# Edge stage of a graph layer: one-hots become the stationary operand of the node sums, messages go in as two exact halves

## What is computed

```
xn   = layernorm(x)
msg  = relu(xn[src] + edge_attr @ W_edge + b_edge)        # 50000 x 256
agg  = segment_sum(msg, dst)                               # 3125 x 256
h    = (1 + eps) * xn + agg
h    = relu(h @ W1 + b1) @ W2 + b2, batch norm, relu
q, k = elu(xn @ Wq.T) + 1, elu(xn @ Wk.T) + 1;  v = xn @ Wv.T
mix  = (q @ (k.T v)) / (q @ sum(k)), projected             # 8 heads
x    = x + h + mix
x    = x + routed_ffn(layernorm(x))                        # 2 of 8 experts per node
```

## Time and profile before

| | |
|---|---|
| median of 3 runs | 1014.85 us (1013.4 to 1015.24) |
| the profiled execution's own time | 1009.37 us |
| its span from first to last instruction | 1007.6 us |
| edge stage, first fetch to `edges_done` | 43.0 to 559.6 us |
| graph layer's rest, routing | 559.6 to about 680 us |
| feed-forward blocks | about 680 us to the end |

### The profile page before, as it was taken

How to read it: one execution, slowest core, us unless ns; L and a number is a source line. 1 busy time by engine, 2 the same in 40 slices (tenths; PEclk the granted TensorE clock), 3 DMA queues, 4 the chain that set the end, 5 groups by cost and what they waited for, 6 DMA issues and landing times.

```text
span 1007.6 us, 17432 instructions
## 1 busy us (share of the span) xinstructions
PE 926.4 (92%) x6055; PEld 824.6 (82%) x6055; DVE 601.8 (60%) x1098; ACT 538.3 (53%) x1064; POOL 544.6 (54%) x527
## 2 busy tenths in 40 slices
PE   5899999999999999999999975379999999999995
PEld 4677889889888888897888765368999999999994
DVE  5555665565665565568989778835554454555442
ACT  2744545445545455445545564836555666555552
POOL 3277777777777777777774004023444444444433
PEclk8899999999999999999999998589999999999998
DMA  9667888877878878799775105459799789888722
GB/s 247 198 165 231 264 259 266 254 253 251 277 243 260 274 252 262 249 304 324 248 241 184 43 1 182 168 201 384 236 312 308 239 289 301 279 253 301 244 42 28
DMA packets 93173, 234.59 MB, mean 233 GB/s; under 512 B 20425, under 2 KB 37843, under 8 KB 84122
## 3 DMA queue, kind: packets, MB, share of 16 engines
q1 hardware_dynamic: 56694, 116.95, 33.9%
q0 software_dynamic: 29136, 64.72, 26.5%
q10 hardware_dynamic: 7252, 51.75, 12.8%
HBM read 183.81 MB, written 50.23 MB: 232 GB/s over the span
## 4 chain that ended last, share of the span: by engine, by line
PE 59%; POOL 13%; DMA 10%; DVE 8%; issue 7%; ACT 2%; DVEq 0%; POOLq 0%; SPq 0%; ACTq 0%
PE banks L1154 15%; POOL work L775 13%; PE banks L1174 10%; DMA work<-node_table,srcT 8%; PE banks L476 7%; PE banks L450 7%; PE banks L1176 5%; PE banks L924 3%; PE banks L983 2%; PE banks L439 2%; PE banks L1063 2%; PE banks L1051 1%; DVE work L526 1%; PE banks L1138 1%; DMA wts<-in_src 1%
## 5 line engine op out<-in xcount | busy, mean ns | idle before, releaser
L775 POOL DMA_INDIRECT work<-node_table,srcT x391 | 382.9, 979 | 151.6 <-issue 109.8
L498 ACT ACTIVATE work<-work 128x512 f32<-128x512 f32 x195 | 120.9, 630 | 127.0 <-DVE work L526 126.3
L476 PEld LDWEIGHTS banks<-work 128*128 128x128 f32 x1560 | 184.2, 192 | 4.5 <-DVE hT L544 1.1
L476 PE MATMUL banks<-work 128*128 128x128 f32 x1560 | 184.8, 275 | 0.7 <-DVE hT L544 0.7
L450 PE MATMUL banks<-w_edge,eaT 128*128 128x256 f32 x780 | 179.1, 379 | 0.0
L526 DVE TENSOR_TENSOR work<-banks,work 128x512 f32<-128x512 f32 x195 | 128.0, 682 | 69.5 <-DMA work<-node_table,srcT 55.1
L824 POOL DMA_INDIRECT out<-work,row_i x54 | 86.5, 1601 | 141.5 <-ACT work L1444 118.9
L1154 PE MATMUL banks<-xe_hi,wup 128*128 128x256 f32 x864 | 158.8, 285 | 3.8 <-DVE xe_lo L1901 3.8
L450 PEld LDWEIGHTS banks<-w_edge,eaT 128*128 128x128 f32 x780 | 143.1, 190 | 17.0 <-issue 0.2
L1174 PE MATMUL banks<-wdown,hid_hi 128*128 x432 | 155.9, 403 | 0.0
L1909 DVE TENSOR_TENSOR hid_lo<-wts,hid_hi 128x512 fp32r<-128x512 f32 x108 | 72.4, 691 | 134.7 <-ACT hid_hi L1421 134.7
(11 more groups left out here) (258 smaller groups left out, 1199.1 us busy)
## 6 DMA issues: line engine op xcount, KB each, us to landing
wup<-split_table ACTq DMA_DIRECT2D x24, 2048.0 KB, 9.7
work<-in_edge_attr SPq DMA_DIRECT2D x65, 384.0 KB, 5.1
wts<-in_L_ffn_W SPq DMA_DIRECT2D x64, 256.0 KB, 4.6
split_table<-raw_hi SPq DMA_DIRECT2D x64, 256.0 KB, 2.6
split_table<-raw_lo SPq DMA_DIRECT2D x64, 256.0 KB, 4.2
wdown<-split_table SPq DMA_DIRECT2D x8, 2048.0 KB, 9.7
work<-node_table,srcT POOLq DMA_INDIRECT x391, 4.5
wup<-split_table SPq DMA_DIRECT2D x3, 2048.0 KB, 8.2
```

The source lines that it names most:

```text
L476: last = nc.tensor.matmul(bank[5][:, h * P:(h + 1) * P], msg[:, u, j, h * P:(h + 1) * P], onehot[:, u, j], start=(j == 0), stop=(j == GT - 1))
L498: nc.scalar.activation(msg[:, u, 2 * q:2 * q + 2], msg[:, u, 2 * q:2 * q + 2], ACT.Relu).then_inc(msg_ready, 1)
L775: pool.indirect_dma_start(out=xg[i % RING][0:rows, j % 2], out_offset=None, in_=node_table, in_offset=bass.IndirectOffsetOnAxis(ap=srcT[0: ...
```

## The change

A one-hot tile is now the stationary operand and the messages of a tile (256 values wide) are the moving one. Both are in the fp32r format: the one-hots are exact in it, and the messages are given as two halves. ACT's relu writes a rounded `msg_hi` to other memory (that of `xs`, which is free in this stage), and a new DVE instruction `low_messages` computes `msg_lo = max(msg, 0) - msg_hi` over the whole group, once ACT is done with all three pairs. PE then runs 12 matmuls of 128x256 (one record each) for a group in place of 24 records of 128x128. The sums now come out node by node where `hT` wants them turned, so ACT copies them to `sums` (`copy_sums`) and PE transposes them (`turn_sums`, two 128x128) before DVE adds them. On ACT the copy of the sums and the mixer's steps come ahead of the edge copy; on DVE `mix_q` comes right behind the one-hots, and `add_window` between the second and the third pair. The loads of x, 10 DMAs, move on SP from n = 51 to 55 to behind `edges_done`, since `xs` now holds messages.

```diff
-        onehot = view(work, 7680, 2, GT, P)
+        msg_lo = nc.alloc_sbuf_tensor_at("msg_lo", [P, 2, GT, DIM], F32R, offset=work_offset + 4 * 4608)
+        msg_hi = nc.alloc_sbuf_tensor_at("msg_hi", [P, 2, GT, DIM], F32R, offset=xs_offset)
+        sums = xs[:, 12]
+        onehot = nc.alloc_sbuf_tensor_at("onehot", [P, 2, GT, P], F32R, offset=work_offset + 4 * 7680)
...
-        def aggregate_tail(pe, n, u):
-            pe.wait_ge(agg_read, n)
-            pe.wait_ge(onehot_ready, n + 1)
-            pe.wait_ge(msg_ready, PAIRS * (n + 1))
-            for h in range(HALVES):
-                last = nc.tensor.matmul(bank[5][:, h * P:(h + 1) * P], msg[:, u, 0, h * P:(h + 1) * P], onehot[:, u, 0],
-                                        start=True, stop=True)
-            last.then_inc(agg_ready, 1)
-
-        def aggregate(pe, n, u, fresh=False):
+        def aggregate(pe, n, u, fresh=False, tiles=GT):
             if not fresh:
                 pe.wait_ge(agg_read, n)
             pe.wait_ge(onehot_ready, n + 1)
+            pe.wait_ge(msg_low, n + 1)
+            for j in range(tiles):
+                for m in (msg_hi, msg_lo):
+                    last = nc.tensor.matmul(bank[5][:, 0:DIM], onehot[:, u, j], m[:, u, j],
+                                            start=(j == 0 and m is msg_hi), stop=(j == tiles - 1 and m is msg_lo))
+            last.then_inc(agg_ready, 1)
+
+        def turn_sums(pe, n):
+            pe.wait_ge(sums_copied, n + 1)
             for h in range(HALVES):
-                for j in range(GT):
-                    if h == 0 and j % 2 == 0:
-                        pe.wait_ge(msg_ready, PAIRS * n + j // 2 + 1)
-                    last = nc.tensor.matmul(bank[5][:, h * P:(h + 1) * P], msg[:, u, j, h * P:(h + 1) * P], onehot[:, u, j],
-                                            start=(j == 0), stop=(j == GT - 1))
-            last.then_inc(agg_ready, 1)
+                last = nc.tensor.transpose(bank[5][:, DIM + h * P:DIM + (h + 1) * P], sums[:, h * P:(h + 1) * P], ident[:])
+            last.then_inc(turned, 1)
...
+        def copy_sums(act, n):
+            act.wait_ge(agg_ready, n + 1)
+            nc.scalar.copy(sums, bank[5][:, 0:DIM]).then_inc(sums_copied, 1)
+
+        def high_tail(act, n, u):
             act.wait_ge(sums_done, PAIRS * (n + 1))
-            nc.scalar.activation(msg[:, u, 0], msg[:, u, 0], ACT.Relu).then_inc(msg_ready, PAIRS)
-
-        def relu_messages(act, n, u):
+            nc.scalar.activation(msg_hi[:, u, 0], msg[:, u, 0], ACT.Relu).then_inc(msg_high, PAIRS)
+
+        def high_messages(act, n, u):
             for q in range(PAIRS):
                 act.wait_ge(sums_done, PAIRS * n + q + 1)
-                nc.scalar.activation(msg[:, u, 2 * q:2 * q + 2], msg[:, u, 2 * q:2 * q + 2], ACT.Relu
-                                     ).then_inc(msg_ready, 1)
+                nc.scalar.activation(msg_hi[:, u, 2 * q:2 * q + 2], msg[:, u, 2 * q:2 * q + 2], ACT.Relu
+                                     ).then_inc(msg_high, 1)
+
+        def low_messages(dve, n, u, tiles=GT):
+            dve.wait_ge(msg_high, PAIRS * (n + 1))
+            nc.vector.scalar_tensor_tensor(out=msg_lo[:, u, 0:tiles], in0=msg[:, u, 0:tiles], scalar=0.0,
+                                           in1=msg_hi[:, u, 0:tiles].bitcast(F32), op0=ALU.max, op1=ALU.subtract
+                                           ).then_inc(msg_low, 1)
...
-        def add_nodes(dve, n, u):
-            for q in range(PAIRS):
+        def add_nodes(dve, n, u, pairs=range(PAIRS)):
+            for q in pairs:
...
-            dve.wait_ge(agg_ready, n + 1)
+            dve.wait_ge(turned, n + 1)
...
+            nc.vector.tensor_tensor(w, bank[5][:, DIM:2 * DIM].rearrange("p (h c) -> p h c", h=HALVES),
...
-                c = n - 2 * TILES - 1
-                if 0 <= c < CHUNKS:
-                    for d, s in node_rows(a["x"], xs[:, c * CHUNK_TILES:(c + 1) * CHUNK_TILES], c):
-                        sp.dma_start(s, d).then_inc(x_again, 16)
...
             sp.wait_ge(edges_done, 1)
+            for c in range(CHUNKS):
+                for d, s in node_rows(a["x"], xs[:, c * CHUNK_TILES:(c + 1) * CHUNK_TILES], c):
+                    sp.dma_start(s, d).then_inc(x_again, 16)
...
+                if n >= 2:
+                    turn_sums(pe, n - 2)
                 if n == DEN0:
                     attn_weights()
-                if n >= 1:
-                    aggregate(pe, n - 1, (n - 1) % 2, n == 1)
                 if n < 2 * TILES:
                     if n % 2 == 0:
                         mix_kv(n // 2)
...
                     context_transpose()
                 if n >= DEN0 and (n - DEN0) % 2 == 0 and (n - DEN0) // 2 < COL_CHUNKS:
                     attn_den((n - DEN0) // 2)
+                if n >= 1:
+                    aggregate(pe, n - 1, (n - 1) % 2, n == 1)
                 if n >= DEN0 + 3 and (n - DEN0 - 3) % 2 == 0:
                     attn_out((n - DEN0 - 3) // 2)
-            aggregate_tail(pe, GROUPS - 1, (GROUPS - 1) % 2)
+            turn_sums(pe, GROUPS - 2)
+            aggregate(pe, GROUPS - 1, (GROUPS - 1) % 2, tiles=1)
+            turn_sums(pe, GROUPS - 1)
...
+            act.wait_ge(rows_ready, CHUNKS)
             for n in range(GROUPS):
-                if n + 1 < GROUPS:
-                    copy_group(n + 1)
+                if n >= 2:
+                    copy_sums(act, n - 2)
                 if 1 <= n <= 2 * TILES:
                     if n % 2 == 1:
                         mix_kv(n // 2)
                     else:
                         mix_q(n // 2 - 1)
+                if n + 1 < GROUPS:
+                    copy_group(n + 1)
                 if n == DEN0:
...
-                    relu_messages(act, n, n % 2)
+                    high_messages(act, n, n % 2)
                 else:
-                    relu_tail(act, n, n % 2)
+                    high_tail(act, n, n % 2)
...
-                    add_window(dve, n - 2, starts[(n - 2) % GT], mixed_by(n + 1), n == 2)
+                    dve.wait_ge(agg_ready, n - 1)
                 if last:
                     mark_tail(dve, n % 2)
                 elif n < 2 or n > 2 * TILES:
...
                     mark_from_psum(dve, n, n % 2)
                 if n % 2 == 1 and n < 2 * TILES:
                     mix_k(n // 2)
+                if n % 2 == 0 and 2 <= n <= 2 * TILES:
+                    mix_q(n // 2 - 1)
                 if n == 2 * TILES:
                     mask_context()
                 c, late = (n - DEN0 - 1) // 2, (n - DEN0 - 1) % 2
                 if 0 <= c < COL_CHUNKS and not last:
                     attn_inverse(c, 2 * late)
+                if not last:
+                    add_nodes(dve, n, n % 2, range(PAIRS - 1))
+                if n >= 2:
+                    add_window(dve, n - 2, starts[(n - 2) % GT], mixed_by(n + 1), n == 2)
                 if last:
                     add_tail(dve, n, n % 2)
                 else:
-                    add_nodes(dve, n, n % 2)
-                if n % 2 == 0 and 2 <= n <= 2 * TILES:
-                    mix_q(n // 2 - 1)
+                    add_nodes(dve, n, n % 2, (PAIRS - 1,))
                 if n >= 1 and (n - 1) % GT == 0:
                     starts = windows_from(n - 1)
                 if n >= 3:
                     round_low(dve, n - 3)
+                low_messages(dve, n, n % 2, 1 if last else GT)```

On DVE, in the mixer's part of the stage, from the end of one group to the end of the next (an odd n), before. `raw_lo` is the weights' low half, `hT<-banks,hT` the window, `work<-banks,relT` the one-hots, `work<-banks,work` the adds:

```order
L587 TENSOR_TENSOR raw_lo_53<-wts,raw_hi_50 128x512
L1571 SCALAR_TENSOR_TENSOR hT<-qT,eps,hT 128x2x125
L544 ISA
L544 TENSOR_TENSOR hT<-banks,hT 128x2x128
L508 TENSOR_TENSOR work<-banks,relT 128x768
L1584 SCALAR_TENSOR_TENSOR k_t<-ek,banks 125x256
L526 TENSOR_TENSOR work<-banks,work 128x512 x3
L587 TENSOR_TENSOR raw_lo_54<-wts,raw_hi_51 128x512
```

More of the change, by code:

```diff
@@ L1321, in _ @@
                     nc.scalar.copy(w2_hi[:], w2[:]).then_inc(w12_high, 1)
+            for n in range(GROUPS - 2, GROUPS):
+                copy_sums(act, n)
             again = act.value_load(miss_i[0:1, 0:1], min_val=0, max_val=1)
@@ L1651, in _ @@
                     round_low(dve, n - 3)
+                low_messages(dve, n, n % 2, 1 if last else GT)
                 if n == 5:
@@ L1689, in _ @@
                         add_nodes_again(dve, n)
+                        low_messages(dve, n, 0)
                         add_window(dve, n, w * WINDOW, TILES)
```

12 lines of the change are left out of this document (8 added, 4 removed).

## The result

The changed kernel takes **1081.35 us** (median of 4 runs, 1079.66 to 1084.63), the one before on the same chip 1014.12 us (4 runs, 1011.92 to 1015.24): a ratio of 1.067, interval 1.0638 to 1.0701. The forecast was 1082 us. The profiled execution took 1079.66 us with a span of 1077.9 us, 70.3 us more than before.

The account below looks back on a forecast made before the run. The prediction took POOL's fetches, not PE, to bound the edge stage. Its terms 51 + 18 - 2 = +67 us on the profiled 1009.37 us made 1076, and 5.5 us to the median made 1082 us; range 1046 to 1108.

Parts of the forecast that it names:

- The bound: Edge stage: POOL's fetches, one every 1.25 us, set the step; PE, 92% busy, runs beside them.
- What holds the fetches: Edge stage: a DVE instruction with both inputs in SBUF holds up a fetch that would start while it runs.
- the term of +51 us: First part, 51 groups: the pass delays fetches 1.00 us a group, the middle of 0.38 to 1.63; bounds +19 and +83.
- +18 for the fetches: Late part, 14 groups: step rises from 7.92 to 9.2 us, +18 us; bounds +16.5 and +23.
- forecast at -2: Last fetch's start to edges_done: 15.7 us becomes about 13.7 by a sum of links; bounds -3 and 0.
- DVE needs 9.1 us: Late part: DVE's 7.35 us of work a group plus the 1.76 us pass, less 0.05 of overlap.
- Almost no idle time: Late part: a sign that would show the forecast's mechanism, DVE left with almost no idle time.
- order on DVE: Edge stage: the new DVE order, with add_window behind two adds, a link under half a step; no cost counted.
- ACT, PE's savings, the loads of x: ACT's 0.37 us copy covered by idle time, PE's 0.8 us a group saved not counted, x loads hidden: 0.
- Rival C: Edge stage: PE's clock falls after pauses, 0.5 us a group, +32 on top, 1114 us; chance 0.05.
- A: First part: the pass does not hold up fetches, only DVE's late load counts, +14.5, 1029 us; chance 0.10.
- B: Edge stage: PE is the bound and gets faster, at most 14 us gained, 1001 us; chance 0.05.

Follow-up runs that it names:

- in thirds: The changed kernel with the pass as three instructions of 512 elements, one behind the other, every value computed: 1050.68 us, ratio 1.0369.
- with a sixth: The changed kernel with the pass over one tile of six, PE using msg_hi again for the other five: 1029.88 us, ratio 1.0149.
- window first: The changed kernel with the window's add, from group 51 on, ahead of the one-hots and adds: 1079.39 us, ratio 1.0637.
- PE filled: The changed kernel with unused matmuls of 128 columns on PE, five or ten a group, so that it pauses less: 1074.41 us, ratio 1.0608.
- sixth and window first: The changed kernel with the pass over one tile of six and, from group 51 on, the window's add ahead: 1023.99 us, ratio 1.0112.
- new until group 50: The changed scheme for groups 0 to 50, the old scheme without the pass from group 51 on: 1052.3 us, ratio 1.0375.
- before with a pass: The old kernel, x loaded late, plus one instruction like the pass on unused memory for groups 2 to 50: 1047.24 us, ratio 1.035.

## Why the prediction was right, point by point

- **The bound** (fetches, not PE): shown for the first part. PE lost 650 records and the time did not fall; in five kernels with PE's new work and a short, divided or PSUM-side pass a group takes 7.66 to 7.78 us there, close to the old 7.65.
- **What holds the fetches**: shown by three kernels from three sides: the input's place (7.66 us), the instruction's length (7.76 us in thirds, 7.70 with a sixth), the instruction alone (+35.1 us). The Trainium skill (SBUF — State Buffer, "Who interferes with whom") says that a DVE instruction with at most one SBUF input outside its two-port modes does not contend with GpSimd; the PSUM input agrees (0.95 us inside the pass). It also infers that descriptor generation isn't held up by a `tensor_tensor`; these fetches are held up by instructions with two SBUF inputs (0.95 us outside, up to 2.48 us inside). Which part of a fetch is held, the reading of its row numbers from SBUF or the making of descriptors, no run shows.
- **Its size**: the term of +51 us measured +40.7. The surplus is 0.80 us a group, not 1.00. The step that failed is taking the middle because landings spread. Of the fetches that start in a pass of the 66 groups, 43 have surpluses of 0.41 to 0.61 us, 18 have 1.02 to 1.53, and two lie between. In 20 of the first part's 51 groups the fetch starts 1.0 to 1.05 us into the pass, so the pass stands in a certain phase to the fetches, and mostly the favourable one. That this comes from landing, add, high half and pass following each other is argued, not shown.
- **The late part**: +18 for the fetches measured +18.5, but this is partly luck, and the end of the stage, forecast at -2, measured +8.7. Together 25.8 us by DVE's own mark for a forecast of 16. The step that failed is "DVE needs 9.1 us", used as the group's step: as busy time it was nearly right (8.87), but it is the step only if every pause closes. "Almost no idle time" was wrong: the old pauses for ACT and landings did shrink, but new ones for PE came, 1.23 us a group in all. The old step plus the pass would be 8.08 + 1.76 = 9.84 for 10.10 measured, but the pass is not the whole cause. With five sixths of it gone (1.34 us) the step falls by 1.01 us only, from 10.10 to 9.09, and 9.2 of the 25.8 us come back. The window's place gives 7.9 more between two traces, and 8.7 are left. The new order and the new links between PE and DVE, which the prediction put at nothing, thus cost about as much here as the pass or more; the node sums' waits for the window name them, but no run takes the link of copy and turns out alone.
- **The end**: the sum of links there took each link as waiting only for the one before it. (The links add up to 12.5 us, not 12.0, which would still be about -2.) Timeline of the changed kernel there:

```profile
609.81 1.09 DVE L1633 SCALAR_TENSOR_TENSOR wts<-wts,qT 128x896 f32<-128x896 f32 x1
...
610.82 0.95 DVE L515 TENSOR_TENSOR onehot<-iota_f,relT 128x768 fp32r<-128x768 f32 x1
611.69 1.55 DVE L1627 RECIPROCAL wts<-wts 128x224 f32<-128x224 f32 x1
613.15 1.22 DVE L539 TENSOR_TENSOR work<-banks,work 128x512 f32<-128x512 f32 x2
...
614.76 0.39 PE L473 MATMUL banks<-msg_hi,onehot 128*128 128x256 f32 x1 [4.21 <-DVE hT L557]
```

  PE waited 4.2 us for a window that stood behind the norm, one-hots, an inverse and two adds. This is the "order on DVE" that was costed at nothing. With a full pass the price of the window's place does not show (window first: 146.2 for 146.4 us); with a short one it is 7.9 us between two traces.
- **ACT, PE's savings, the loads of x**: nothing, as forecast. ACT's copy made PE wait 0.9 us in the late part and the end.
- **Rival C**: its mechanism came true and its price did not. The clock fell to 0.96 and 0.89 in the two parts. With PE filled it was 0.98 and 0.97, and the median 6.9 us lower, not 32; how much of that is the clock's is open.
- **Rivals A and B**: out. A's first part of 7.65 us is approached (7.66 to 7.78) only when the input is in PSUM or the pass is short or divided; B needed a pass that costs less than 0.2 us a group.

The total is nearer than its parts: 10 us too much in the first part, some 11 too little in the late one and the end, 2.5 us elsewhere that was put at nothing. The last step to the median added 5.5 us to the profiled execution's time; in the changed kernel the two are 1.7 us apart. That 1082 lies within 1 us of 1081.35 is luck; the mechanism of the first part and the direction of the whole are not. What stays open: why filled matmuls on PE lower the fetches' surplus by 6 us, and what makes up the last 8.7 us between "sixth and window first" (129.3 us) and the old kernel (120.6). By the step that kernel is 0.36 us a group above the old one with 0.42 us of pass added (8.86 for 8.50), and its DVE waits about 1 us a group for the turns.

## What to carry to other kernels

Where a queue of GpSimd-issued fetches sets the step, price each DVE instruction with two SBUF inputs by what is left of it when a fetch comes: keep it shorter than the fetch's own step, cut it into pieces, or have one input in PSUM. Ask for the phase before taking a mean. When work goes to an engine that is 88% busy in order, do not count on its pauses to close: add the work to its step unless you can name the pause that it fills. Price the new waits between the engines besides: with five sixths of the pass gone the late part and the end still took 16.6 us more than before.

## What the runs showed of the hardware

A DVE instruction is not lengthened by a fetch that started ahead of it: the pass at 303.87 us above starts while a fetch runs (until 304.60) and takes 1.76 us; only the fetch that comes later waits. The division by inputs runs through the changed kernel's whole trace. Fetches that start well inside an instruction with at most one input in SBUF take 0.91 to 0.95 us: 20 in the reciprocals, 53 in the adds of a bank and rows, 24 in the one-hots made from a bank. Those inside one with both inputs there take more: 32 in the weights' low half 0.98 to 1.43 us, two in the late one-hots, made from SBUF alone, 1.13 and 1.47.

Cutting the instruction is enough for a fetch to slip in, with no pause between the pieces (the fetch at 304.42 us above ends at 305.67, inside the row of thirds that ends at 306.06).

In all five kernels whose first part has the full pass or its like (after, new until group 50, window first, PE filled, before with a pass), each fetch that starts well inside it, from 0.06 us after its start to 0.2 us before its end, lasts until 0.81 to 0.83 us after the pass.

The same pause does not always cost the clock. PE paused 3.67 us both before 555.60 and before 573.83 us. After the first the matmuls of the node sums follow each other every 0.12 us:

```profile
556.05 0.28 PE L473 MATMUL banks<-msg_lo,onehot 128*128 128x256 f32 x1
556.17 0.28 PE L473 MATMUL banks<-msg_hi,onehot 128*128 128x256 f32 x1
...
557.13 3.17 PE L995 MATMUL banks<-wts,attn_w 128*128 128x448 f32 x8
...
573.83 0.38 PE L473 MATMUL banks<-msg_hi,onehot 128*128 128x256 f32 x1 [3.67 <-DVE hT L557]
...
574.73 0.41 PE L473 MATMUL banks<-msg_lo,onehot 128*128 128x256 f32 x1
574.94 0.41 PE L473 MATMUL banks<-msg_hi,onehot 128*128 128x256 f32 x1
...
576.22 3.90 PE L995 MATMUL banks<-wts,attn_w 128*128 128x448 f32 x8
```

After the second they come every 0.21 us, and the attention's output behind them takes 3.90 us instead of 3.17. The granted clock was 1.00 from 555.60 to 557.10 us and 0.60 from 573.80 to 576.20, near the lower level of 1.2 GHz. Neither trace nor run shows why the two differ.
